# Weight maxima through TensorE instead of POOL, x tiles loaded first, and a loop jump at another place

## The chip, the cores and the metric

The kernel runs on one core of one Trainium2 chip. The metric is the device time of one execution in microseconds (us); the time given is the median of three runs. Profiles come from one execution taken by the hardware profiler. The core has five engines with queues of their own: TensorE (PE, with its weight loads as PEld), VectorE (DVE), ScalarE (ACT), GpSimd (POOL) and SyncE (SP), which here only issues DMAs. Engines wait for one another on semaphores.

## What is computed

```python
def reference(x, w_qkv, w_out, b_out, w_gate, w_up, w_down):      # x: (8, 1024, 512)
    xn = layernorm(x)
    return x + attn(xn, w_qkv, w_out, b_out) + ffn(xn, w_gate, w_up, w_down)

def attn(x, ...):                       # 8 heads of 64, windows of 4 tokens, stride 2
    win = (x @ w_qkv)[:, idx]           # idx: window starts 0, 2, 4, ... plus 0..3
    q, k, v = split(win)
    o = softmax(q @ k.T * C ** -0.5) @ v          # inside each window and head
    return scatter_add(zeros, idx, o @ w_out + b_out)

def ffn(x, ...):                        # 512 -> 1408 -> 512
    gate, up = fp4_linear(x, w_gate), fp4_linear(x, w_up)
    return fp4_linear(silu(gate) * up, w_down)
    # fp4_linear rounds both operands to FP4 (E2M1) in blocks of 16 with a scale per block
```

## The kernel before

x is 8 batches of 8 tiles of 128 tokens. The first part of the program makes the attention, batch by batch, and prepares the FFN's weights beside it; the second part makes the FFN, 64 tiles in one pipeline. The products of the projections take f16 pairs: an operand is split into a high and a low half, and three products (high-high, high-low, low-high) stand for one. One projection step is 12 products of 512 columns.

**The order** of each engine's work is a string of steps, written out by hand or by a planner: `q3` is step q number 3 of the present batch, `q3+` the same of the next batch, `q3'` of the previous one. `batches` (line 116) follows four strings: a head, then a loop of six turns whose body is two of the strings, then a tail. Where the body ends, the engine jumps back. Every engine has its own strings; they meet only in semaphores.

**Steps on TensorE:** `q` and `v` project q/k and v (L970, L977, products at L960), `s` makes scores of three tiles (L1004), `a` attends (L1021), `p` projects out (`prj`, L960), `F` is a third of the gate and up products of the first FFN tile, `W` waits until w_out and the edge rows are ready. The `q` and `v` steps go through three PSUM buffers `acc`, so each needs ACT's copy of the third step before it.

**VectorE:** `t` statistics of an x tile (L691, L694), `n` normalisation (L780), `Q` maximum over one of four row blocks of w_qkv (L650), `W0` maximum over the four (L639), `W1` the gain from it (`weight_gain`, L629 to L633), `V` low half of a sixth of the weights (L657), `U` the same three steps for w_out, `M` maxima of the nine chunks of the FFN's weights (L819), `G` their gains, `m`, `c`, `k`, `u`, `z` the softmax of three tiles, `w` the transposition of the spread weights (L749), `A`, `R` rounding of FFN weights, `I`, `J` rounding of the first FFN rows.

**ACT:** `x` high half of a normalised tile, `W` high half of a sixth of the weights (L863), `q`, `v` copies from PSUM (L884, L891), `e` exponential, `o` and `h` attention output. The first copy waits for all six `V`, since the raw weights lie in `qk`.

**POOL:** `r` the root of four tiles' variances (L538 and after), `l` low half of a tile, `w` spreading of weights (L561), `b` bias, `o` low half of the output, `C` loads of constants. `W` and `T` are the all-reduces: a maximum lies in one number per partition after VectorE, and `partition_all_reduce` (L528, L601) brings the maximum over all 128 partitions into each.

**SP:** `l` load of an x tile, `k` store of a normalised one, `t` transposing DMA of a tile's halves into `xt`, `C` w_out, `M` a chunk of FFN weights, `e` edge rows, `r`, `s` residual and output. The four parts of w_qkv are issued from ACT's queue, at its start.

Of the kernel before, what the change touches and what calls it, by code (L numbers as in the profile page):

```python
# [8 lines left out]
ALU = mybir.AluOpType  # L9
# [6 lines left out]
P = 128  # L16
# [242 lines left out]
def attention(nc, ctx, x, w_qkv, w_out, b_out, w_gate, w_up, w_down, small, part, normed, ready, late, wsc, raw,  # L259
# [48 lines left out]
    tops = sb("tops", [P, 9])  # L308

# [76 lines left out]
    def sync(sp):  # L386
# [109 lines left out]
        def first_edge(b, n):  # L496
# [15 lines left out]
                {"l": load, "k": keep, "e": edge_values, "r": residual, "s": store,  # L512
                 "L": load_unit, "S": keep_unit, "M": load_maxima, "Z": load_ready,
                 "C": load_out_weights, "W": first_edge, "I": first_rows, "t": turn_rows, "T": turn_unit, "X": turn_first})
    def gpsimd(pool):

        def load_constants(b, n):
            if n == 0:
                pool.dma_start(cst[:, :], small).then_inc(c_in, 16)
# [5 lines left out]
        def all_max(b, n):  # L525

            pool.wait_ge(w_max, n)
            pool.partition_all_reduce(sc[:, 2 * n - 1:2 * n], sc[:, 2 * n - 2:2 * n - 1], P,  # L528
                                      bass.bass_isa.ReduceOp.max).then_inc(w_all, 1)
            if n == 2:  # L530
                pool.wait_ge(bias_set, 3)
# [73 lines left out]
        batches(pool,  # L605
# [800 lines left out]
```

## Time and profile before

| | |
|---|---|
| median of 3 runs | 2263.82 us (2260.72 to 2269.66) |
| the profiled execution's own time | 2262.21 us |
| its span | 2260.4 us |
| granted TensorE clock, mean | 0.988 |
| TensorE busy | 2171.7 us, 96 % |
| VectorE, ACT, POOL busy | 72 %, 29 %, 54 % |
| attention | up to about 890 us |
| FFN | from there to the end |

The span runs from the first to the last recorded instruction. The clock is given as a share of 2.4 GHz; 0.50 is 1.2 GHz. A group of equal instructions in a timeline is one row, with its start, the time to the end of the last, the count, and in brackets the idle time ahead of it with what ended it. "issue" stands where nothing in the profile ended it. A float32 product shows as two instructions in the trace, so a score step of 96 products has 192 rows' worth of instructions, and an attend step of 16 has 32.

### The profile page before, as it was taken

The numbers are of one execution on the slowest core, as the hardware profiler recorded it, in microseconds if no ns is written. First come the engines' busy times: TensorE is split into PE (matmuls) and PEld (weight loads), VectorE is DVE, ScalarE is ACT, GpSimd is POOL, SyncE is SP. The second block draws the span as 40 slices with busy tenths as digits, with TensorE's granted clock in tenths as the row PEclk, the third lists the DMA queues.
The fourth block names the chain that finished last, engine by engine and source line by source line (L and its number), as shares of the span: only waits on it lengthen the run. The fifth ranks groups of instructions, "written<-read, shape, count | busy, mean of one in ns | idle before, by whom it ended". The sixth has DMA issues, their size and how long they took to land.

```text
span 2260.4 us, 46863 instructions
## 1 busy us (share of the span) xinstructions
PE 2171.7 (96%) x16704; PEld 1048.6 (46%) x16704; DVE 1637.1 (72%) x3099; ACT 655.9 (29%) x1009; POOL 1217.9 (54%) x880
## 2 busy tenths in 40 slices
PE   3899999999999998999999999999999999999999
PEld 1444444444445444444444444444444444444444
DVE  6587676766767555777778778778778778778774
ACT  2233333332333322222222222222222222222221
POOL 2166566665756445555555555555555555555553
PEclk9999999999999999999999999999999999999999
DMA  7656465655656635333433433333333333333432
GB/s 221 183 127 182 120 177 135 152 142 136 167 123 176 148 104 192 75 79 79 94 80 78 92 81 80 89 81 83 87 84 82 85 83 79 89 81 76 94 69 70
DMA packets 449389, 251.84 MB, mean 111 GB/s; under 512 B 367266, under 2 KB 373922, under 8 KB 449268
## 3 DMA queue, kind: packets, MB, share of 16 engines
q1 hardware_dynamic: 448404, 245.94, 44.6%
q10 hardware_dynamic: 576, 3.15, 0.3%
q8 instruction: 101, 1.65, 0.3%
q0 software_dynamic: 288, 0.94, 0.2%
q14 instruction: 20, 0.16, 0.0%
HBM read 98.98 MB, written 59.77 MB: 70 GB/s over the span
## 4 chain that ended last, share of the span: by engine, by line
PE 88%; issue 5%; DVE 3%; POOL 1%; DMA 1%; ACT 1%; SPq 0%; DVEq 0%; ACTq 0%; POOLq 0%
PE acc L960 19%; PE prj L1316 7%; PE ops L1316 7%; PE prj L960 6%; PE acc L1297 5%; PE acc L1298 5%; PE acc L1301 5%; PE ops L1318 3%; PE prj L1318 3%; PE acc L1299 2%; PE acc L1300 2%; PE acc L1302 2%; PE sps L1302 2%; PE sps L1300 2%; PE sps L1299 2%
## 5 line engine op out<-in xcount | busy, mean ns | idle before, releaser
L960 PE MATMUL acc<-late 128*128 128x512 f16 x2304 | 536.3, 390 | 61.0 <-DVE late L657 33.5
L960 PEld LDWEIGHTS acc<-late 128*128 128x128 f16 x2304 | 223.9, 100 | 339.6 <-issue 92.5
L208 POOL TENSOR_TENSOR qk<-qk,xh 128x1408 f32<-128x1408 f32 x64 | 165.6, 2588 | 230.1 <-DVE qk L245 230.1
L203 POOL TENSOR_TENSOR qk<-qk,xh 128x1024 f32<-128x1024 f32 (+1 forms) x128 | 177.3, 1385 | 111.2 <-DVE xh L224 111.2
L213 POOL TENSOR_TENSOR v<-qk,v 128x1408 f16<-128x1408 f32 x64 | 183.0, 2859 | 100.3 <-ACT v L255 100.3
L1191 DVE SCALAR_TENSOR_TENSOR qk<-acc,row_gains,xh 128x512 f32<-128x512 f32 x64 | 48.0, 750 | 253.1 <-ACT xh L1256 253.1
L1316 PE MATMUL prj<-late,qk 128*128 128x512 f16 x704 | 214.6, 379 | 0.7 <-DMA qk<-v 0.7
L1316 PE MATMUL ops<-late,qk 128*128 128x512 f16 x704 | 214.6, 379 | 0.0
L1297 PE MATMUL acc<-late,turned 128*128 128x512 f16 x512 | 194.4, 380 | 3.0 <-DVE qk L1191 3.0
L255 ACT ACTIVATE v<-qk 128x1408 f16<-128x1408 f32 x64 | 88.1, 1377 | 367.4 <-POOL qk L208 367.4
L1298 PE MATMUL acc<-late,turned 128*128 128x512 f16 x512 | 194.4, 380 | 0.0
L1301 PE MATMUL acc<-late,turned 128*128 128x512 f16 x512 | 194.3, 380 | 0.0
L960 PE MATMUL prj<-wo,oh 128*128 128x512 f16 x768 | 176.3, 379 | 4.8 <-DVE res L773 3.7
L250 ACT ACTIVATE qk<-qk 128x1024 f32<-128x1024 f32 (+1 forms) x128 | 101.1, 790 | 226.5 <-POOL qk L203 226.5
L208 POOL TENSOR_TENSOR raw<-raw,scales 128x512 f32<-128x512 f32 x64 | 67.8, 1060 | 141.7 <-DVE raw L245 141.7
L1318 PE MATMUL prj<-late,qk 128*128 128x512 f16 x352 | 133.5, 379 | 0.0
L1318 PE MATMUL ops<-late,qk 128*128 128x512 f16 x352 | 133.4, 379 | 0.0
L553 POOL TENSOR_TENSOR res<-res,bias 128x512 f32<-128x512 f32 x64 | 83.3, 1305 | 66.9 <-DMA res<-in_L_attn_x 66.8
L1256 ACT ACTIVATE xh<-acc,row_gains 128x512 f32<-128x512 f32 x128 | 83.7, 677 | 121.5 <-PE sps L1302 120.3
L884 ACT ACTIVATE qk<-acc 128x512 f32<-128x512 f32 x128 | 74.8, 593 | 148.0 <-PE acc L960 143.7
L245 DVE SCALAR_TENSOR_TENSOR qk<-qk 128x1024 f32<-128x1024 f32 (+1 forms) x128 | 114.1, 891 | 4.4
L960 PEld LDWEIGHTS prj<-wo,oh 128*128 128x128 f16 x768 | 73.2, 98 | 93.0 <-issue 5.7
(150 smaller groups left out, 4422.5 us busy)
## 6 DMA issues: line engine op xcount, KB each, us to landing
late<-in_L_attn_x SPq DMA_DIRECT2D x64, 256.0 KB, 3.8
normed<-late SPq DMA_DIRECT2D x64, 256.0 KB, 3.0
res<-in_L_attn_x SPq DMA_DIRECT2D x64, 256.0 KB, 3.1
attended<-res SPq DMA_DIRECT2D x64, 256.0 KB, 2.5
raw<-normed SPq DMA_DIRECT2D x64, 256.0 KB, 2.7
v<-attended SPq DMA_DIRECT2D x64, 256.0 KB, 2.7
out<-v SPq DMA_DIRECT2D x64, 256.0 KB, 2.0
ready<-turned SPq DMA_DIRECT2D x36, 256.0 KB, 2.7
```

What stands on the lines that cost most here:

```text
L203: pool.tensor_tensor(blocks(v), blocks(v), spread(s[2]), ALU.mult).then_inc(q["scaled"], 1)
L208: pool.tensor_tensor(blocks(v), blocks(v), spread(s[3]), ALU.mult).then_inc(q["valued"], 1)
L213: pool.tensor_tensor(h[:, 1], v, h[:, 0], ALU.subtract).then_inc(q["low"], 1)
L245: dve.scalar_tensor_tensor(v, m, ROUND_MIN, v, ALU.max, ALU.subtract).then_inc(q["rounded"], 1)
L250: act.activation(m, v, ACT.Abs, scale=ROUND_Y).then_inc(q["rounder"], 1)
L960: last = pe.matmul(out, lhsT, rhs, start=(at == 0), stop=(at == n - 1))
L1297: pe.matmul(g, x_hi, g_hi, start=(c == 0), stop=False)
L1298: pe.matmul(g, x_hi, g_lo, start=False, stop=False)
L1299: pe.matmul(w, x_hi, u_hi, start=(c == 0), stop=False)
L1301: pe.matmul(g, x_lo, g_hi, start=False, stop=(c == KC - 1))
L1316: last = pe.matmul(dps[k][:, :], ht[:, k, at], w_hi, start=(at == 0), stop=(at == 2 * FC - 1))
L1318: pe.matmul(dps[k][:, :], ht[:, k, at], w_lo, start=False, stop=False)
```

## The change

1. The maximum over partitions is made by TensorE. VectorE multiplies an identity by the column of 128 partial maxima (`diag`), TensorE multiplies a matrix of ones by that diagonal, which puts all 128 numbers side by side into every partition of `prj`, and VectorE reduces them there. So it is for w_qkv (`M0`), w_out (`M1`) and the two FFN maxima (`M2`). POOL has no all-reduce any more. New: `eye` (loaded by POOL at its start), `ones`, `diag`.
2. ACT's queue starts with x tiles 2 and 3 and two of the four parts of w_qkv; SP's queue loads tiles 0, 1, 4 and 5, then stores the first normalised tile, then loads the other two parts (`Q`).
3. The semaphores' first increments are made by POOL and not by TensorE.
4. All heads and tails have a new order. The loop's body is the same sequence on each engine; TensorE's jump back stands ahead of `q3+` instead of ahead of `q5+`.

```diff
@@ sync
+        def load_weights(b, k):
+            sp.dma_start(wqs[:, k], w_qkv[k * P:(k + 1) * P, :]).then_inc(w_in[k], 16)
-                "l0 l1 l2 l3 k0 l4 l5 l6 l7 t0 t1 t2 t3 k1 k2 k3 C0 M0 M1 t4 t5 l0+ l1+ M2 M3 t6 k4 l2+ l3+ M4 t7 M5 "
+                "l0 l1 l4 l5 k0 Q2 Q3 l6 t0 t1 l7 t2 t3 k1 C0 M0 M1 l0+ t4 k2 l1+ l2+ l3+ l4+ k3 k4 k5 t5 t6 M2 t7 M3 "
@@ gpsimd
+                pool.dma_start(eye[:, :], ident).then_inc(c_in, 16)
-        def all_max(b, n):
-            pool.wait_ge(w_max, n)
-            pool.partition_all_reduce(sc[:, 2 * n - 1:2 * n], sc[:, 2 * n - 2:2 * n - 1], P,
-                                      bass.bass_isa.ReduceOp.max).then_inc(w_all, 1)
-        def all_tops(b, n):
-            for n in range(2):
-                pool.wait_ge(m_top, n + 1)
-                pool.partition_all_reduce(wsc[:, 2 + n:3 + n], wsc[:, n:n + 1], P,
-                                          bass.bass_isa.ReduceOp.max).then_inc(m_all, 1)
+        for q, n in per_batch.items():
+            pool.sem_inc(q, n)
@@ vector
+        dve.memset(ones[:, :], 1.0).then_inc(half_set, 1)
         def weight_gain(n):
+            at_ = n // 2 * P
             dve.wait_ge(w_all, (n + 1) // 2)
+            link(dve.tensor_reduce(sc[:, n:n + 1], prj[:, at_:at_ + P], AX.X, ALU.max))
@@ weights, n == 0
                 dve.wait_ge(wq_max, KC)
-                dve.tensor_reduce(sc[:, 0:1], sc[:, 16:20], AX.X, ALU.max).then_inc(w_max, 1)
+                dve.tensor_reduce(sc[:, 0:1], sc[:, 16:20], AX.X, ALU.max).then_inc(wq_max, 1)
+                dve.wait_ge(c_in, 32)
+                dve.wait_ge(wq_max, KC + 1)
+                dve.tensor_scalar(diag[:, 0], eye[:, :], sc[:, 0:1], None, ALU.mult).then_inc(w_max, 1)
...
+        def unit_tops(b, n):
+            dve.wait_ge(m_done, 9)
+            dve.wait_ge(w_all, 2)
+            for n, cols in enumerate((slice(0, 6), slice(6, 9))):
+                dve.tensor_reduce(wsc[:, n:n + 1], tops[:, cols], AX.X, ALU.max).then_inc(m_step, 1)
+                dve.wait_ge(m_step, n + 1)
+                dve.tensor_scalar(diag[:, n], eye[:, :], wsc[:, n:n + 1], None, ALU.mult).then_inc(m_top, 1)
@@ scalar
-        for k in range(KC):
+        for i in range(2, 4):
+            act.dma_start(xb[:, i, :], x_t[i]).then_inc(x_in[i], 16)
+        for k in range(2):
             act.dma_start(wqs[:, k], w_qkv[k * P:(k + 1) * P, :]).then_inc(w_in[k], 16)
@@ tensor
-        for q, n in per_batch.items():
-            pe.sem_inc(q, n)
+        def column_tops(b, n):
+            if n < 2:
+                pe.wait_ge(half_set, 2)
+                pe.wait_ge(w_max, n + 1)
+                pe.matmul(prj[:, n * P:(n + 1) * P], ones[:, :], diag[:, n], start=True, stop=True).then_inc(w_all, 1)
+            else:
+                pe.wait_ge(m_top, 2)
+                for m in range(2):
+                    pe.matmul(prj[:, (2 + m) * P:(3 + m) * P], ones[:, :], diag[:, m],
+                              start=True, stop=True).then_inc(m_all, 1)
-                "q0 q1 q2 q3 q4 q5 q6 q7 v0 s0 v1 v2 v3 q8 q9 q10 q11 q12 q13 q14 q15 v4 v5 s1 a0 v6 v7 a1 s2 a2 q0+ "
-                "q1+ q2+ q3+ q4+ a3 W0",
-                "p6' v4 s1 a0 v5 a1 p7' v6 s2 v7 a2 q0+ q1+ q2+ a3 q3+ q4+",
-                "q5+ a4 q6+ q7+ v0+ p0 a5 v1+ s0+ p1 a6 v2+ p2 a7 v3+ q8+ q9+ q10+ q11+ p3 q12+ q13+ p4 a8 q14+ p5 "
+                "M0 q0 q1 q2 q3 q4 q5 q6 q7 v0 v1 v2 M1 s0 v3 q8 q9 q10 q11 q12 q13 q14 q15 v4 v5 s1 a0 M2 v6 v7 a1 "
+                "s2 a2 q0+ q1+ q2+ W0 a3",
+                "p6' v4 s1 a0 v5 a1 p7' v6 s2 v7 a2 q0+ q1+ q2+ a3",
+                "q3+ q4+ q5+ a4 q6+ q7+ v0+ p0 a5 v1+ s0+ p1 a6 v2+ p2 a7 v3+ q8+ q9+ q10+ q11+ p3 q12+ q13+ p4 a8 "
```

TensorE's queue, from its start to the loop (`L119` is the loop's entry; L960 and L1004 are products of projections and scores, L1021 of attending). Before:

```order
L960 MATMUL acc<-late 128x512 x108
L1004 MATMUL sps<-qk 32x32 x96
L960 MATMUL acc<-late 128x512 x156
...
L1021 MATMUL ops<-pt,v 64x64 x16
L960 MATMUL acc<-late 128x512 x24
L1021 MATMUL ops<-pt,v 64x64 x16
L1004 MATMUL sps<-qk 32x32 x96
L1021 MATMUL ops<-pt,v 64x64 x16
L960 MATMUL acc<-late 128x512 x60
L1021 MATMUL ops<-pt,v 64x64 x16
L119 UNCONDITIONAL_BRANCH
```

The same stretch of the changed kernel, where L977, L1021 and L1038 are those lines and L1054, L1058 the products with ones:

```order
L1054 MATMUL prj<-diag,ones 128x128
L977 MATMUL acc<-late 128x512 x132
L1054 MATMUL prj<-diag,ones 128x128
L1021 MATMUL sps<-qk 32x32 x96
L977 MATMUL acc<-late 128x512 x132
...
L1038 MATMUL ops<-pt,v 64x64 x16
L1058 MATMUL prj<-diag,ones 128x128 x2
L977 MATMUL acc<-late 128x512 x24
...
L1038 MATMUL ops<-pt,v 64x64 x16
L977 MATMUL acc<-late 128x512 x36
L1038 MATMUL ops<-pt,v 64x64 x16
L119 UNCONDITIONAL_BRANCH
```

The score step s0 moved behind two more projection steps, four products with ones came in, and 24 products (q3+, q4+) left the stretch between the second `s2` and the loop.

POOL's queue at its start (L538 is the root, L547 a low half, L528 the all-reduce, L519 and L522 loads). Before:

```order
L538 TENSOR_SCALAR ln<-mv 128x4
L540 TENSOR_TENSOR ln<-ln,sc 128x4
L543 TENSOR_SCALAR ln<-ln 128x4
L547 TENSOR_TENSOR xh<-late,xh 128x512 x4
L519 DMA cst<-in_small 128x291
L528 ISA
L528 ISA sc<-sc 128x1
L522 DMA bias<-in_L_attn_b_out 128x512 x3
L538 ISA
L538 TENSOR_SCALAR ln<-mv 128x4
```

The changed kernel:

```order
L525 DMA eye<-in_ident 128x128
L526 DMA cst<-in_small 128x291
L541 ISA
L541 TENSOR_SCALAR ln<-mv 128x4
L543 TENSOR_TENSOR ln<-ln,sc 128x4
L546 TENSOR_SCALAR ln<-ln 128x4
L550 TENSOR_TENSOR xh<-late,xh 128x512 x3
L529 DMA bias<-in_L_attn_b_out 128x512 x3
L550 TENSOR_TENSOR xh<-late,xh 128x512
L541 TENSOR_SCALAR ln<-mv 128x4
```

Between the first root and the second there is no all-reduce and no `ISA` step any more, and the constants are loaded ahead of the first root.

## Rows read from the trace of the kernel before

**Rows 1.** The page's first part: an engine's busy time, share, instructions.

```profile
PE 2171.7 (96%) x16704; PEld 1048.6 (46%) x16704; DVE 1637.1 (72%) x3099; ACT 655.9 (29%) x1009; POOL 1217.9 (54%) x880
```

**Rows 2.** Waits of TensorE: waiter, releaser, us in total, times, longest.

```profile
PE acc L960 <- DVE late L657: 33.5, 1, 33.5
PE acc L960 <- issue: 23.8, 8, 4.1
PE sps L1004 <- issue: 8.8, 7, 1.7
```

**Rows 3.** Timeline, 12 to 63 us: start, length, engine, instruction, count, idle before.

```profile
12.73 0.69 DVE L691 BATCH_NORM_STATS2 st<-late 128x6 f32<-128x512 f32 x1 [1.55 <-DMA late<-in_L_attn_x]
13.57 0.18 DVE L694 BATCH_NORM_AGGREGATE mv<-st 128x2 f32<-128x6 f32 x1
16.11 0.55 DVE L780 TENSOR_SCALAR late<-late,mv,ln 128x512 f32<-128x512 f32 x1 [0.72 <-POOL ln L543]
19.67 3.40 DVE L650 TENSOR_REDUCE sc<-qk 128x1 f32<-128x1536 f32 x2
24.85 0.12 DVE L639 TENSOR_REDUCE sc<-sc 128x1 f32<-128x4 f32 x1
29.56 0.38 POOL L528 PARTITION_ALL_REDUCE sc<-sc  x1 [5.77 <-issue]
31.94 7.24 DVE L657 SCALAR_TENSOR_TENSOR late<-qk,sc,late 128x1024 f16<-128x1024 f32 x6
33.45 12.51 PE L960 MATMUL acc<-late 128*128 128x512 f16 x48 [33.45 <-DVE late L657]
45.30 0.25 POOL L538 TENSOR_SCALAR ln<-mv 128x4 f32<-128x4 f32 x1 [13.65 <-issue]
49.55 13.11 PE L960 MATMUL acc<-late 128*128 128x512 f16 x60 [3.59 <-ACT qk L884]
```

**Rows 4.** Timeline, 69 to 110 us.

```profile
69.57 35.46 PE L960 MATMUL acc<-late 128*128 128x512 f16 x151 [3.97 <-issue]
92.40 0.54 DVE L780 TENSOR_SCALAR late<-late,mv,ln 128x512 f32<-128x512 f32 x1 [4.33 <-POOL ln L543]
93.92 1.75 DVE L819 TENSOR_REDUCE tops<-ot 128x1 f32<-128x1536 f32 x1
108.76 0.71 DVE L749 STREAM_TRANSPOSE pt<-pw 128x512 f32<-128x512 f32 x1 [6.06 <-POOL pw L561]
109.62 1.13 PE L1021 MATMUL ops<-pt,v 64*64 64x64 f32 x32 [2.84 <-DVE pt L749]
```

**Rows 5.** Timeline of TensorE in the loop's first and third turn.

```profile
214.03 2.66 PE L1004 MATMUL sps<-qk 64*32 64x32 f32 x190
218.36 0.29 PE L1004 MATMUL sps<-qk 64*32 64x32 f32 x2 [1.68 <-issue]
218.59 4.35 PE L960 MATMUL acc<-late 128*128 128x512 f16 x12
241.43 4.45 PE L960 MATMUL acc<-late 128*128 128x512 f16 x12 [4.08 <-issue]
...
419.09 1.67 PE L960 MATMUL acc<-late 128*128 128x512 f16 x7 [0.33 <-issue]
...
430.35 0.24 PE L1004 MATMUL sps<-qk 64*32 64x32 f32 x2 [0.93 <-issue]
430.53 2.76 PE L960 MATMUL acc<-late 128*128 128x512 f16 x12
```

**Rows 6.** The page's DMA queues (packets, MB, share) and issues (KB each, us to landing).

```profile
q8 instruction: 101, 1.65, 0.3%
late<-in_L_attn_x SPq DMA_DIRECT2D x64, 256.0 KB, 3.8
```

**Rows 7.** Busy time of each engine in a stretch, then granted clock, DMA share, GB/s.

```profile
219.00:221.00 2.00, 2.00 (x6) 0.73 (x5) 0.00 (x0) 0.00 (x0) 0.54 (x1) 0.50 1.03 262
```

**Rows 8.** Timeline of TensorE at the start of the FFN.

```profile
914.37 0.38 PE L1297 MATMUL acc<-late,turned 128*128 128x512 f16 x1 [3.04 <-DVE qk L1191]
```

More of the change, by code:

```diff
@@ L255, in high, with attention @@
     act.activation(h[:, 0], v, ACT.Copy).then_inc(q["high"], 1)
-def attention(nc, ctx, x, w_qkv, w_out, b_out, w_gate, w_up, w_down, small, part, normed, ready, late, wsc, raw,
+def attention(nc, ctx, x, w_qkv, w_out, b_out, w_gate, w_up, w_down, small, ident, part, normed, ready, late, wsc, raw,
               rows, shared, held):
@@ L663, in out_weights @@
                 dve.wait_ge(o_in, 16)
-                dve.tensor_reduce(sc[:, 2:3], wos, AX.XY, ALU.max, apply_absolute_value=True).then_inc(w_max, 1)
+                dve.tensor_reduce(sc[:, 2:3], wos, AX.XY, ALU.max, apply_absolute_value=True).then_inc(wq_max, 1)
+                dve.wait_ge(wq_max, KC + 2)
+                dve.tensor_scalar(diag[:, 1], eye[:, :], sc[:, 2:3], None, ALU.mult).then_inc(w_max, 1)
             if n == 1:
@@ L681, in fixed_values @@
             else:
-                dve.wait_ge(c_in, 16)
+                dve.wait_ge(c_in, 32)
                 dve.wait_ge(b_in, 48)
@@ L819, in maxima @@
             dve.tensor_reduce(tops[:, n:n + 1], v, AX.XY, ALU.max, apply_absolute_value=True).then_inc(m_done, 1)
+        def unit_tops(b, n):
[5 more added lines that the diff above has]
+                dve.tensor_scalar(diag[:, n], eye[:, :], wsc[:, n:n + 1], None, ALU.mult).then_inc(m_top, 1)
         def unit_gains(b, n):
-            dve.wait_ge(m_done, 9)
-            dve.tensor_reduce(wsc[:, 0:1], tops[:, 0:6], AX.X, ALU.max).then_inc(m_top, 1)
-            dve.tensor_reduce(wsc[:, 1:2], tops[:, 6:9], AX.X, ALU.max).then_inc(m_top, 1)
             dve.wait_ge(m_all, 2)
+            for n in range(2):
+                dve.tensor_reduce(wsc[:, 2 + n:3 + n], prj[:, (2 + n) * P:(3 + n) * P], AX.X, ALU.max)\
+                    .then_inc(m_step, 1)
+            dve.wait_ge(m_step, 4)
+            dve.wait_ge(m_top, 2)
             dve.tensor_scalar(wsc[:, 0:2], wsc[:, 2:4], 1.0 / 6.0, 1e-12, ALU.mult, ALU.max).then_inc(m_step, 1)
-            dve.wait_ge(m_step, 1)
+            dve.wait_ge(m_step, 5)
             dve.tensor_scalar(wsc[:, 2:4].bitcast(I32), wsc[:, 0:2].bitcast(I32), 0x7F800000, None,
                               ALU.bitwise_and).then_inc(m_step, 1)
-            dve.wait_ge(m_step, 2)
+            dve.wait_ge(m_step, 6)
             dve.reciprocal(wsc[:, 6:8], wsc[:, 2:4]).then_inc(m_step, 1)
@@ L850, in vector @@
                  "A": unit_scales, "R": round_unit,
-                 "M": maxima, "G": unit_gains, "W": weights,
+                 "M": maxima, "G": unit_tops, "H": unit_gains, "W": weights,
                  "Q": weights_top, "V": weights_low, "U": out_weights, "Z": fixed_values,
@@ L1035, in out_ready @@
             pe.wait_ge(ve_zero, 16)
+            pe.wait_ge(m_step, 4)
         def first_products(b, n):
@@ L1041, in tensor @@
         batches(pe,
-                "q0 q1 q2 q3 q4 q5 q6 q7 v0 s0 v1 v2 v3 q8 q9 q10 q11 q12 q13 q14 q15 v4 v5 s1 a0 v6 v7 a1 s2 a2 q0+ "
-                "q1+ q2+ q3+ q4+ a3 W0",
-                "p6' v4 s1 a0 v5 a1 p7' v6 s2 v7 a2 q0+ q1+ q2+ a3 q3+ q4+",
-                "q5+ a4 q6+ q7+ v0+ p0 a5 v1+ s0+ p1 a6 v2+ p2 a7 v3+ q8+ q9+ q10+ q11+ p3 q12+ q13+ p4 a8 q14+ p5 "
-                "q15+",
-                "q5 q6 a4' q7 a5' v0 v1 p0' s0 p1' v2 p2' a6' v3 q8 p3' q9 q10 a7' q11 q12 q13 q14 a8' p4' q15 v4 p5' "
-                "s1 v5 v6 a0 s2 a1 p6' v7 a2 p7' a3 a4 F0 a5 p0 p1 a6 p2 a7 p3 a8 p4 p5 p6 p7 F1 F2",
-                {"q": project_qk, "v": project_v, "s": scores, "a": attend, "p": project_out, "W": out_ready,
+                "M0 q0 q1 q2 q3 q4 q5 q6 q7 v0 v1 v2 M1 s0 v3 q8 q9 q10 q11 q12 q13 q14 q15 v4 v5 s1 a0 M2 v6 v7 a1 "
+                "s2 a2 q0+ q1+ q2+ W0 a3",
+                "p6' v4 s1 a0 v5 a1 p7' v6 s2 v7 a2 q0+ q1+ q2+ a3",
+                "q3+ q4+ q5+ a4 q6+ q7+ v0+ p0 a5 v1+ s0+ p1 a6 v2+ p2 a7 v3+ q8+ q9+ q10+ q11+ p3 q12+ q13+ p4 a8 "
+                "q14+ p5 q15+",
+                "q3 q4 q5 q6 q7 a4' v0 v1 p0' s0 p1' a5' v2 v3 q8 a6' p2' a7' q9 p3' a8' q10 q11 q12 p4' q13 q14 q15 "
+                "v4 a0 v5 a1 s1 p5' v6 v7 s2 a2 p6' a3 a4 p7' a5 p0 p1 a6 p2 a7 p3 a8 p4 p5 p6 p7 F0 F1 F2",
+                {"q": project_qk, "v": project_v, "s": scores, "a": attend, "p": project_out, "M": column_tops, "W": out_ready,
                  "F": first_products})
@@ L1356, in build @@
         held = sem("held")
-        att, ended = attention(nc, ctx, x, w_qkv, w_out, b_out, w_gate, w_up, w_down, small, part, normed, ready, late,
+        att, ended = attention(nc, ctx, x, w_qkv, w_out, b_out, w_gate, w_up, w_down, small, ident, part, normed, ready, late,
                                wsc, raw, rows, shared, held)
```

15 lines of the change are left out of this document (8 added, 7 removed), and 34 rows, old and new, of tables (dst, to, v).

## The prediction

> **What bounds the kernel now.** I read the busy line first, then TensorE's waits, then the timeline from the start, then the places where TensorE stops. TensorE is busy 2171.7 us of 2260.4 [rows 1]. Of what is left, 33.5 us stand before the first product, 23.8 us in 8 stops with no releaser ("issue"), 8.8 us in 7 more such stops at the scores [rows 2]. So a microsecond counts only where it takes a TensorE stop away or adds one; the other engines matter where they end such a stop. There are three kinds.
>
> *The start.* Ahead of TensorE's 33.45 stand, one after another: the fourth tile's statistics (end 13.75), the first normalisation at 16.11, the weight reductions, the one over all four at 24.97, POOL's all-reduce, over at 29.94, and the split of the weights from 31.94 [rows 3]. From 24.97 to 29.94 nothing but the all-reduce is on this path: 5.0 us.
>
> *POOL behind an all-reduce.* Its next ordinary step, root 1, comes at 45.30 after 13.65 us with no releaser. So tile 4 is normalised late, ACT has its step x4 ahead of the copies, and TensorE waits 3.59 us at 49.55 [rows 3]. Behind the third all-reduce VectorE waits 6.06 us for POOL's spreading and turns the weights at 108.76, for which TensorE waits 2.84 us at 109.62 [rows 4].
>
> *Stops with no releaser.* Five, the first of 4.08 us, stand at the loop's jump, ahead of q5. Six stand in s2, each after 190 of its 192 rows, the first of 1.68 and the third of 0.93 us [rows 5], 7.8 us in all. They recur at one instruction, so they hang on the program's place in memory and not on data. The page has a queue for instructions with 101 packets and 1.65 MB, 16.3 KB each [rows 6]. I take an instruction as 64 bytes, which makes a packet a block of 256; that is inferred, and this is its test. A row of the timeline is two instructions, load and product. From the stop at 419.09, after 5 of v5's 12 products, to the one at 430.35, after 190 rows of s2 [rows 5], there are 7 + 32 + 12 + 12 + 190 = 253 rows, 506 instructions, and 7 waits and register steps: 513, two blocks and one. The stop at 69.57 [rows 4], after 5 products of v1, lies 13 x 256 ahead of the one at 419.09 by the same count. So TensorE stops where two block borders follow each other faster than a block arrives. In s2 they are 128 rows apart, 1.8 to 1.9 us at its rate (190 rows in 2.66); with the stops of 0.93 to 1.68 a block takes 2.8 to 3.5 us.
>
> *The clock.* From 219 to 221 the granted clock is 0.50, that is 1.2 GHz [rows 7], behind the stop of 1.68, and v7's 12 products take 4.35 us; behind that of 0.93 they take 2.76 [rows 5]. Such a fall costs 1.6 us.
>
> **The change, part by part.** *x ahead of weights.* An x tile lands 3.8 us after its issue [rows 6], so the first at 4.6; VectorE takes about 1.0 a tile (12.73 to 13.75), and the first normalisation was 2.36 behind the fourth aggregate [rows 3]: 4.6 + 4.0 + 2.4 = 11. Four of them take 2.1 (0.55 each), four weight reductions 6.8 (3.40 for two): 20. SP now issues two of the four weight parts behind the first normalised tile, at 12. They are three x tiles' bytes each; between 3.8 and three times that I take 6, so they are there at 18, and at worst at 23. Tile 6 ends at 21, the reduction over all with it; before, 24.97.
>
> *TensorE for POOL.* The 5.0 us become a 128x128 multiply, one f32 product and one reduction from PSUM. No row shows these; the nearest are VectorE's 128x512 step of 0.55 and its 128x1536 reduction of 1.7, and f16 products of 0.23 to 0.36. With their semaphores I bound the three by 0.8 and 2.5 us. They lie beside tile 7's statistics and root 1, for the first split now has tile 4's normalisation ahead of it: tile 7 at 22.3 to 23, 2.36 to the root's end, 0.55 for tile 4, makes 25.2 to 25.9 against 31.94. I take 25.9: **6.0 us**, 3 (late weights) to 7.
>
> *No reload on POOL.* Root 1 comes at once and x4 is past before the first copy, so the 3.59 goes. At a0 the spreading comes straight behind VectorE's first group, some 30 us ahead of TensorE: the 2.84 goes. **6.4 us**, and 1.6 of a clock fall behind the latter, of which I take **0.8**. What is late next there: TensorE's queue now holds M1 ahead of s0 and M2 behind a0, and it waits in them for VectorE, with v6, v7, a1, s2 and all later work queued behind M2. M1 comes at 62.66 (49.55 + 13.11) - 9.6 + 5.2 = 58; the w_out maximum it needs is eleven short steps behind the last split (39.18 before, 33 now): by 48. M2 comes at 109.62 - 12 = 98; the ninth maximum ends at 95.67 even with today's order, and VectorE stood still for POOL for 4.33 us shortly ahead of it [rows 4]: about 88. The products and their weight loads cost 0.1 to 0.9 us each, three of them on the path: a loss of **1.0**.
>
> *The stop of 3.97 in the head* [rows 4]: the borders now fall 128 rows before the end of s0 and at its end, without the 5 products between. It becomes 1.0 (a block in 2.8) to 5.1 (as slow as now): no change taken.
>
> *The loop.* Every engine keeps its order; TensorE's jump alone moves, from behind q4 to behind a3. The head has 24 products less, POOL does the increments for TensorE, and the M products come in. Counted in the built program, the loop's top goes from instruction 2240 to 2158, and q5, s2 and all else of the body to 28 instructions earlier. The border that lay 4 instructions before s2's end falls 24 behind it, after 11 of v7's 12 products. Between it and the one before lie 117 rows of s2, 1.6 us, and 11 products, 2.4 us: 4.0 us where a block takes 2.8 to 3.5. So **the six stops of s2 go, 7.8 us**, and with them falls of the clock. The two rows behind such stops show 1.6 and none; for the six I take four falls, 6.4, less 1.5 since the jump's stop may now be the one that halves it for longer: **4.9**. The jump's stop stays: its target block must still come. Sum 12.7, 7 (clock as now) to 15.
>
> *The tail.* F0, which filled TensorE between a4 and a5, moves behind p7, and VectorE prepares the first rows of FFN earlier. The last and largest of the tail's stops is 3.04, in the first FFN tile [rows 8]. F0's 24 products, 5.2 us, are missing as filler, while VectorE has some 5 us less between s2 and a6, and the 3.04 gets more work ahead of it: a gain of 1 to 4. Against it, by the count, s0 and s1 of the tail now hold two borders each, 128 rows apart, where none did: 2 x 1.4 us and up to two falls of the clock, 3.2. Net a **loss of 2**, from a gain of 3 to a loss of 6.
>
> **Sum.** 6.0 + 6.4 + 0.8 - 1.0 + 12.7 - 2.0 = 22.9 off the profiled run's 2262.21 us (its span is 2260.4) gives 2239.3. That run is 1.6 under the median of the runs, 2263.82, so the same off the median is 2240.9.
>
> The Trainium skill's page "Runtime: NRT & Kernel Launch", section "Instruction fetch mechanics", has blocks of 16 KiB, 256 instructions, whose fetch is mostly hidden behind issue, and a stall where a taken branch leaves the window. The packets of rows 6 and the stop at the jump agree with it. The stops in s2 speak against "hidden", as nothing branches there; taken at its word they have another cause and stay, which is rival 1.
>
> The Trainium skill's page "GPSIMD Engine Reference", section "Instruction dispatch", states about 6 us ahead of a freshly loaded kernel's first call. The 5.0 us ahead of the first all-reduce are near that; the 13.65 behind it are twice as long, and the sum goes by the rows.
>
> **Rivals.** (1) *The s2 stops are no borders, or do not move.* The loop gives nothing, the tail's new stops do not come either: 6.0 + 6.4 + 0.8 - 1.0 + 1 = 13 off, 2251. For it: the block is inferred. Against: three kinds of stops at whole multiples of 256. (2) *The head's gain is lost again*, at M1, M2 or through late weights: TensorE is 12 us ahead there, and VectorE has to be so too. With the loop's gain alone: 10.7 off, 2253. (3) *The jump's block comes slowly.* The jump moves 5 us forward, into a stretch with transfers under way. If the block takes as in the head, 3.97 + 1.8 + 1.1 = 6.9 us, the five stops grow by 3.4 each, with falls of the clock by 5: 1 off, 2263. (4) *Slower: M2 waits.* Its place is TensorE's queue behind a0; each us that the ninth maximum ends after 98 costs one. Its loads wait in turn for reductions, SP has edge rows and transposes between them, and VectorE waits at the w_out gain for M1. Against 22.9 it makes the kernel slower than now from 121, by over 0.5 % from 132, which gives 2275. Against it: 95.67 today.
>
> **How the numbers follow.** Forecast with its ends, 2231 to 2249: 0.62. More gain: 0.04. Rival 1, 2249 to 2254: 0.16. Rival 2, 2250 to 2256: 0.10. Rival 3: 0.05. Rival 4: 0.03. An effect of 0.5 % is 11.3 us, about what a measurement of this kernel can tell from no change; faster is below 2252.5. Of rival 1 three quarters lie there, of rival 2 half: 0.62 + 0.04 + 0.12 + 0.05 = 0.83, same 0.14, slower 0.03. The range 2230 to 2254 leaves out about 0.15.
>
> **What the profile after must show.** TensorE's first product with weights at 26 to 29; no stop of 3.6 at the first copies and none at a0, which comes at about 98; no 13 us gap on POOL. In the loop no stop in s2, and one of 3.7 to 4.1 at the jump, ahead of q3. In the tail one stop inside s0 and one inside s1, so the stops at scores sum to about 5 us, not 8.8. Wrong would be a wait at M1 or M2, or s2's stops still at 190 of 192.

## The result, and the profile after

The changed kernel takes **2241.03 us** (median of 4 runs, 2238.1 to 2243.07) against 2264.56 for the kernel before, ratio 0.9901 with a 95% interval of 0.9879 to 0.9923. The prediction said 2241. Its profiled run took 2239.38 us with a span of 2237.6, against 2262.21 and 2260.4. Of the four executions each of two kernels further down, one with the jump back (2292.88) and one with the late bias loads (3253.32) ran slower at a lower granted clock; they count in those medians and not in the ratios.

The total came as forecast, the parts did not. I cut both spans at the same three places of TensorE: its first product with weights, attend a4 of the head, and attend a4 of the tail. Tail and FFN stay one row, since the change moves F0 from one to the other. "Stopped" is the stretch less TensorE's busy time in it.

| stretch | before | after | difference | of it stopped | of it busy | forecast |
|---|---|---|---|---|---|---|
| to the first product | 33.45 | 35.96 | +2.5 | | | -6.0 |
| head, to a4 | 105.21 | 96.59 | -8.6 | -6.7 | -2.0 | -6.2 |
| loop, a4 to a4 | 633.12 | 618.08 | -15.0 | -7.6 | -7.4 | -12.7 |
| tail and FFN | 1488.6 | 1487.0 | -1.7 | +1.6 | -3.3 | +2.0 |
| sum | | | -22.8 | | | -22.9 |

The page's first line (busy us, share of the span, instructions) and TensorE's waits (waiter, releaser, us in total, times, longest), which answer to [rows 1] and [rows 2]:

```profile
PE 2159.8 (97%) x16712; PEld 1048.1 (47%) x16712; DVE 1640.4 (73%) x3108; ACT 655.2 (29%) x1009; POOL 1216.9 (54%) x877
```

```profile
PE acc L977 <- issue: 22.9, 6, 4.4
PE prj L1054 <- DVE diag L643: 22.8, 1, 22.8
PE acc L977 <- DVE late L661: 12.4, 1, 12.4
...
PE ops L1038 <- issue: 3.8, 2, 2.3
...
PE sps L1021 <- issue: 2.3, 1, 2.3
```

TensorE's busy time fell by 12 us although its record has 8 rows more, those of the four products with ones. Its mean granted clock rose from 0.988 to 0.994, so most of that is half-clock time that is gone. The stops at the scores went from 8.8 us in 7 to 2.3 in one; those ahead of the large products hardly moved (23.8 to 22.9). The start, in the timeline (start, length, engine, line, operation, count, idle time before and what ended it), answers to [rows 3]:

```profile
14.44 5.76 SPq L408 DMA_TRANSPOSE late<-xh  x2
20.25 0.58 SPq L395 DMA_DIRECT2D late<-in_L_attn_x  x1
21.01 9.59 SPq L408 DMA_TRANSPOSE late<-xh  x2
```

```profile
22.15 0.12 DVE L640 TENSOR_REDUCE sc<-sc 128x1 f32<-128x4 f32 x1
22.38 0.29 DVE L643 TENSOR_SCALAR diag<-eye,sc 128x128 f32<-128x128 f16 x1
30.92 0.69 DVE L697 BATCH_NORM_STATS2 st<-late 128x6 f32<-128x512 f32 x1 [8.25 <-DMA late<-in_L_attn_x]
...
31.85 0.26 DVE L629 TENSOR_REDUCE sc<-prj 128x1 f32<-128x128 f32 x1
```

The maxima are spread as meant: diagonal at 22.38, product, one reduction. But VectorE stands 8.25 us ahead of that reduction for the eighth x tile. Its load was issued at 20.25, behind two transposing DMAs that took 5.76 us to issue. Next the head behind it, answering to [rows 4]:

```profile
35.96 30.22 PE L977 MATMUL acc<-late 128*128 128x512 f16 x132 [12.38 <-DVE late L661]
66.02 0.38 PE L1054 MATMUL prj<-diag,ones 128*128 128x128 f32 x2
66.33 1.82 PE L1021 MATMUL sps<-qk 64*32 64x32 f32 x192
70.42 30.07 PE L977 MATMUL acc<-late 128*128 128x512 f16 x132 [2.27 <-issue]
...
102.41 0.69 PE L1038 MATMUL ops<-pt,v 64*64 64x64 f32 x32
103.03 0.71 PE L1058 MATMUL prj<-diag,ones 128*128 128x128 f32 x4
...
114.06 0.56 PE L1038 MATMUL ops<-pt,v 64*64 64x64 f32 x13 [2.27 <-issue]
```

No stop at the first copies, none at a0, no wait at M1 or M2. The stop behind s0 is 2.27 instead of 3.97, and the one inside a2 is 2.27 instead of 0.69. The loop's first turn answers to [rows 5]:

```profile
207.40 2.83 PE L1021 MATMUL sps<-qk 64*32 64x32 f32 x192
210.16 2.76 PE L977 MATMUL acc<-late 128*128 128x512 f16 x12
...
221.36 0.69 PE L1038 MATMUL ops<-pt,v 64*64 64x64 f32 x32
226.44 4.02 PE L977 MATMUL acc<-late 128*128 128x512 f16 x10 [4.39 <-issue]
```

s2 runs through, in every turn; the jump, now ahead of q3, has its stop: 4.39, 4.08, 4.11, 4.01 and 4.08 us in the five times that it is taken. Five such stops, 20.7 us, are nearly all that TensorE stands still in the loop (618.08 less 597.05 busy). In the tail there is one stop in s1 and none in s0, and the FFN's first one, [rows 8], is 0.44 instead of 3.04:

```profile
812.26 0.26 PE L1021 MATMUL sps<-qk 64*32 64x32 f32 x5 [2.32 <-issue]
...
893.14 0.38 PE L1327 MATMUL acc<-late,turned 128*128 128x512 f16 x1 [0.44 <-DVE qk L1221]
```

So two questions stood: why the start was 8.5 us later than forecast, and whether the program's place in memory is really what makes the stops.

### The profile page after: what moved, and what is told of

The parts are those of the page before. It is cut to its first block, busy times and chain, and to the rows that moved or that the text cites. A ratio compares the mean times of both kernels' runs of the same rounds, so it can differ in the third digit from the quotient of the medians.

```text
span 2237.6 us, 46878 instructions
## 1 busy us (share of the span) xinstructions
PE 2159.8 (97%) x16712; PEld 1048.1 (47%) x16712; DVE 1640.4 (73%) x3108; ACT 655.2 (29%) x1009; POOL 1216.9 (54%) x877
## 4 chain that ended last, share of the span: by engine, by line
PE 94%; DVE 2%; issue 2%; DMA 1%; ACT 0%; POOL 0%; SPq 0%; DVEq 0%; ACTq 0%; POOLq 0%
PE acc L977 23%; PE prj L977 7%; PE prj L1346 7%; PE ops L1346 7%; PE acc L1327 5%; PE acc L1328 5%; PE acc L1331 5%; PE ops L1348 3%; PE prj L1348 3%; PE sps L1021 2%; PE sps L1332 2%; PE acc L1332 2%; PE sps L1330 2%; PE acc L1330 2%; PE acc L1329 2%; PE sps L1329 2%
## 5 line engine op out<-in xcount | busy, mean ns | idle before, releaser
L977 PE MATMUL acc<-late 128*128 128x512 f16 x2304 | 526.1, 387 | 35.3 <-issue 22.9
L977 PEld LDWEIGHTS acc<-late 128*128 128x128 f16 x2304 | 223.3, 99 | 307.3 <-issue 54.9
L977 PE MATMUL prj<-wo,oh 128*128 128x512 f16 x768 | 176.3, 379 | 5.7 <-DVE res L779 5.7
L550 POOL TENSOR_TENSOR xh<-late,xh 128x512 f16<-128x512 f32 x64 | 77.0, 1213 | 101.6 <-ACT xh L894 101.5
L977 PEld LDWEIGHTS prj<-wo,oh 128*128 128x128 f16 x768 | 73.2, 98 | 93.7 <-issue 5.5
```

What stands on the lines that cost most here:

```text
L977: last = pe.matmul(out, lhsT, rhs, start=(at == 0), stop=(at == n - 1))
```

## Experiments

All ratios are against the kernel before in the same comparison, with 95% intervals. "Waits" are waits of TensorE on a semaphore that has long been set; they only move the rest of its program on. The built program keeps half of the repeated ones: 228 written move it by 114 instructions, 60, 28 and 28 by 30, 14 and 14, and the traces hold just so many instructions more (46977 against 46863; 46908, 46892 and 46892 against 46878). My first two expectations had counted all of them.

### The kernel before, its program moved on

```diff
+        for _ in range(228):
+            pe.wait_ge(half_set, 1)
```

> The kernel before, with 228 waits that are already fulfilled put at the start of TensorE's queue, where it stands idle for 33 us. All else is the kernel before. They move every later TensorE instruction 228 on in memory, which is 28 back against block borders of 256, as the change does. If the stops in s2 come from two borders 128 rows apart (theory of borders): no stop at row 190 of s2 in the six turns, turns of about 103 us instead of 105.5, the first weight product still at 33.5, and the whole 12 to 16 us faster than the kernel before, ratio 0.993 to 0.995. If they come from the data, from the jump's place or from what runs beside s2 (rival): stops where they were, ratio 1.000 within 0.002.

Measured: 2276.14 us, ratio 1.0077 (1.0055 to 1.0098). The direction was missed. TensorE's waits, and one stop of the second turn:

```profile
PE sps L1006 <- issue: 39.9, 19, 3.4
```

```profile
256.44 2.00 PE L1006 MATMUL sps<-qk 64*32 64x32 f32 x180
261.09 0.28 PE L1006 MATMUL sps<-qk 64*32 64x32 f32 x12 [2.64 <-issue]
```

The stops behind row 190 of s2 are gone, and others stand in s0 behind row 180 and in s1 behind row 174, of every turn. With the shift corrected to 114, the same count of 256 instructions puts two borders 128 rows apart there, so that two steps of a turn have a stop instead of one. One place does not fit: the border at row 190 of s2 should have moved to row 133, 128 rows behind another, and in the six turns s2 has no stop but one of 0.23 us. So the count places the stops that came, while two borders 128 rows apart did not always make one; why not there, no run shows. And a second thing: the stop at the jump, 4.08 us in [rows 5], is gone (one of 0.40 is the largest that I read there). Nothing at the jump had been touched, so the jump's stop depends on place as well, which the prediction had not thought of.

### The changed kernel, its program moved on

```diff
+        for _ in range(28):
+            pe.wait_ge(half_set, 1)
```

> The changed kernel with 28 fulfilled waits at the start of TensorE's queue, where it stands idle. Borders fall 28 instructions earlier in the work, so that in the loop they are where they were before the change. Theory of borders: in each turn a stop of 0.9 to 1.7 us after 190 of 192 rows of s2, with falls of the clock, turns of about 105 us, and 12 to 16 us more than the changed kernel: ratio to the kernel before 0.995 to 0.997. Rival (the jump's place, ahead of q3, took the stops away): no stop in s2, ratio 0.990.

Measured: 2243.26 us, ratio 0.9924 (0.9905 to 0.9943), which overlaps that of the changed kernel; its profiled span is 2234.2. The expectation was missed: 14 instructions are too few to bring a border back into s2. By the count the border comes to lie in v7, the step behind s2, after 4 of its 12 products, and there the stops are, 0.21 to 0.95 us in the six turns:

```profile
310.48 1.04 PE L979 MATMUL acc<-late 128*128 128x512 f16 x4
312.24 1.89 PE L979 MATMUL acc<-late 128*128 128x512 f16 x8 [0.72 <-issue]
```

### The jump back where it was

```diff
-                "s2 a2 q0+ q1+ q2+ W0 a3",
-                "p6' v4 s1 a0 v5 a1 p7' v6 s2 v7 a2 q0+ q1+ q2+ a3",
-                "q3+ q4+ q5+ a4 q6+ q7+ ...",
-                "q3 q4 q5 q6 q7 a4' v0 ...",
+                "s2 a2 q0+ q1+ q2+ W0 a3 q3+ q4+",
+                "p6' v4 s1 a0 v5 a1 p7' v6 s2 v7 a2 q0+ q1+ q2+ a3 q3+ q4+",
+                "q5+ a4 q6+ q7+ ...",
+                "q5 q6 q7 a4' v0 ...",
```

> The changed kernel with the jump of TensorE back ahead of q5: q3+ and q4+ stand in the head and at the body's end. The order of the work is the same in every engine, and s2 keeps its place against the borders within 4 instructions. Theory of borders: the jump's place is worth nothing, ratio 0.990 within 0.001, no stop in s2, five stops of about 4 us ahead of q5. Rival (moving the jump gave the gain of the loop, 15 us): ratio 0.996.

Measured: **2222.76 us**, ratio 0.9839 (0.9782 to 0.9895), outside both of the ranges that I had put down. The timeline of TensorE at the first jump:

```profile
216.50 5.35 PE L977 MATMUL acc<-late 128*128 128x512 f16 x24
222.39 2.76 PE L977 MATMUL acc<-late 128*128 128x512 f16 x12 [0.53 <-issue]
```

The two loops, of the changed kernel and of this one (stretch, us, busy us of TensorE, granted clock, DMA share, GB/s):

```profile
132.55:750.63 618.08, 597.05 (x7513) 0.98 0.61 152
```

```profile
127.22:723.51 596.29, 589.26 (x7513) 1.00 0.63 158
```

Of the 21.8 us that are gone, 14.0 are stopped time and 7.8 busy time, at a granted clock of 1.00 instead of 0.98. So the same jump costs 3.7 to 4.1 us in the kernel before, 4.0 to 4.4 in the changed kernel, and here at most 0.6. That gave a **new theory**: a jump's stop has two causes. Behind a3's last product the first block of the target takes 4.4 us to be there (221.36 + 0.69 to 226.44). With q3 and q4 ahead of the jump, 5.35 us of products cover that. But if a border comes right behind the loop's first instruction, a second block is needed at once, and the cover is too short for both. Counted in the built programs, the loop's first instruction stands 2 instructions ahead of a border in the kernel before, 144 in the first experiment, 32 here, 84 in the changed kernel.

### Two tests of that theory

First, back behind the large products as here, but moved on by 30 instructions, so that 2 instructions are left to the border as in the kernel before:

```diff
+        for _ in range(60):
+            pe.wait_ge(half_set, 1)
```

> The kernel with the jump put back behind the large products, and TensorE's program moved on by 15 instructions more than one (60 fulfilled waits, of which the built program keeps 30), so that the first instruction of the loop again stands 2 instructions ahead of the border of a block, as in the kernel before, and the borders in the turns again stand where they stood in it. Theory A (a jump's stop has two causes: a block that lies beyond a border just behind the loop's first instruction, and large products missing ahead of the jump to cover the fetch): the stop at the jump returns, 3.5 to 4.1 us in each of 6 turns, and s2's stop after 188 to 190 rows, 1.3 to 1.7 in each turn; 6 x (3.8 + 1.4) = 31 us on jump_back's 2222.8, so 2250 to 2256, ratio 0.994 to 0.998. Theory B (it was only the step that the jump stands ahead of): no stop at the jump, ratio 0.984 to 0.988 with s2's stops alone.

Measured: 2251.32 us, ratio 0.9971 (0.9952 to 0.9991), as theory A said.

```profile
206.85 2.72 PE L1023 MATMUL sps<-qk 64*32 64x32 f32 x190
211.15 0.25 PE L1023 MATMUL sps<-qk 64*32 64x32 f32 x2 [1.58 <-issue]
...
224.84 5.35 PE L979 MATMUL acc<-late 128*128 128x512 f16 x24
233.98 5.30 PE L979 MATMUL acc<-late 128*128 128x512 f16 x12 [3.79 <-issue]
```

Both kinds of stops of the kernel before are back at their rows: at the five jumps 3.79, 3.31, 4.70, 3.25 and 3.87, and behind row 190 of s2 six of 0.99 to 1.58. Fulfilled waits ahead of all work, which do nothing, cost 28.6 us by the medians, 1.3% by the ratios.

Second, the kernel before with the jump's place as the only edit:

```diff
-                "q1+ q2+ q3+ q4+ a3 W0",
-                "p6' v4 s1 ... q0+ q1+ q2+ a3 q3+ q4+",
-                "q5+ a4 q6+ ...",
-                "q5 q6 a4' q7 ...",
+                "q1+ q2+ a3 W0",
+                "p6' v4 s1 ... q0+ q1+ q2+ a3",
+                "q3+ q4+ q5+ a4 q6+ ...",
+                "q3 q4 q5 q6 a4' q7 ...",
```

> The kernel before with one part of the change alone: the jump of TensorE's loop ahead of q3 (behind attend a3) instead of ahead of q5. The loop's first instruction comes to stand 54 ahead of a border instead of 2; the borders within the turns stay where they were. Theory A: the cover is gone (a3's small products take 0.7 us) while the border is no longer near, so one stop takes the place of the other: 3.8 to 4.5 us ahead of q3, s2's stops stay at 1.3 to 1.7, ratio 0.999 to 1.003. Theory B (only the border just behind the loop's first instruction makes the stop): no stop at the jump, 6 x 4.1 = 24.5 us less, ratio 0.988 to 0.990.

Measured: 2265.44 us, ratio 1.0031 (1.0011 to 1.0052); theory B is out.

```profile
236.98 0.69 PE L1021 MATMUL ops<-pt,v 64*64 64x64 f32 x32
241.75 9.54 PE L960 MATMUL acc<-late 128*128 128x512 f16 x36 [4.07 <-issue]
```

One cause took the place of the other: 3.42 to 4.07 us at each of the five jumps, where it had been 3.69 to 4.08 with a border behind the loop's first instruction.

A look at the size: jump back, and 18 instructions left to the border.

```diff
+        for _ in range(28):
+            pe.wait_ge(half_set, 1)
```

> jump_back with TensorE's program moved on by 14 instructions (28 fulfilled waits, of which the built program keeps half): the loop's first instruction stands 18 ahead of a border, between jump_back's 32 (stops of 0.3 to 0.7) and jump_back_shifted's 2 (3.3 to 4.7). If the products between the loop's first instruction and the border cover the second block's fetch, 7 products of 0.22 us less stand there than at 32: the stops at the jump are 1.5 to 2.3 us; the span 2212.9 plus 6 x 1.4 = 2221. If the effect has a threshold instead, they are as at 32 or as at 2.

```profile
220.86 6.93 PE L979 MATMUL acc<-late 128*128 128x512 f16 x31
228.74 1.24 PE L979 MATMUL acc<-late 128*128 128x512 f16 x5 [0.94 <-issue]
```

Measured, in one execution: 2222.28 us, span 2220.1. The 31 products are q3, q4 and 7 of q5's 12: behind every jump TensorE runs 7 products into q5 and stops there, 0.94, 1.82, 1.82, 1.27 and 0.99 us, which is the border itself, seen in the trace. In four of the turns a further 0.5 to 1.0 stands ahead of q5. Together they are 0.9 to 2.9 us, where I had expected 1.5 to 2.3; they lie between those of the other two places, so at this one place neither of the two sizes of a threshold came.

The stops can also be laid beside the transfers of instructions, since the trace has a time for every packet of queue q8 of [rows 6]. Inside the stop at the first jump it has one, in the kernel before (237.35 to 241.43):

```profile
q8 instruction: 1, 0.02, 2.2%
```

and in the changed kernel (222.05 to 224.40; from there to 226.44 it has none):

```profile
q8 instruction: 1, 0.02, 3.3%
```

In the kernel before the packet in the stop, from 238.50 to 239.93, is the second behind the jump: the first runs from 234.44 to 236.30, while q3 and q4 still multiply. In the changed kernel the first, from 223.32 to 224.56, stands in the stop itself. With the jump back it runs from 219.51 to 220.39, beneath q3 and q4 (216.50 to 221.85). These are the two causes of the theory. And it holds for all stops: up to 900 us, the profiles of the thirteen kernels have 136 stops of TensorE of 0.9 us or more with no releaser, and each of them ends 1.2 to 2.1 us after a packet of this queue has landed. Only about 11% of the time lies so behind a packet. So they are waits for instructions on their way.

### The start: what made x7 late

The queues from 20 to 32 us, of the changed kernel (packets, MB, share of the 16 engines' time), and the median landing there of the transposing DMAs, 12.5 us against 4.0 in the kernel before:

```profile
q1 hardware_dynamic: 3923, 1.21, 65.9%
q0 software_dynamic: 240, 0.79, 46.6%
...
late<-xh SPq DMA_TRANSPOSE x3, 12.5
```

The queue q0 carries POOL's three bias loads, which the change issues at 16.62 and the kernel before at 29.82. They broadcast one row to 128 partitions. Two edits tell the bias loads and the issue order of SP apart:

```diff
-                "C0 r0 l0 l1 l2 C1 l3 r1 l4 l5 ...      (POOL)
+                "C0 r0 l0 l1 l2 l3 r1 l4 C1 l5 ...
```

> The changed kernel with POOL's three bias loads behind its low half of tile 4 instead of behind that of tile 2. In the changed kernel x tile 7, behind two transposing DMAs, lands 10.6 us after its issue and holds the weights' gain until 31.75. Theory A: the bias loads (0.79 MB in small packets, 47 % of the DMA engines from 20 to 32 us) crowd out the transposes; without them tile 7 is there at 22 to 24, TensorE's first weight product at 26 to 28 instead of 35.96, and the whole 7 to 10 us faster than the changed kernel, ratio 0.986 to 0.987. Theory B: the transposes are slow beside any transfer, tile 7 at 28 or later, gain under 3 us, ratio 0.989 to 0.990.

```diff
-                "l0 l1 l4 l5 k0 Q2 Q3 l6 t0 t1 l7 t2 t3 ...      (SP)
+                "l0 l1 l4 l5 k0 Q2 Q3 l6 l7 t0 t1 t2 t3 ...
```

> The changed kernel with one edit of order: SP issues the load of the eighth x tile ahead of the first two transposing DMAs; the bias loads stay where the change put them. Theory A (x7 was late because its issue stood behind 5.8 us of transposing issues): VectorE's wait of 8.25 for it falls to 2 to 3 and the first weight product comes at 29 to 31; ratio 0.987 to 0.990. Theory B (it was late because the bias loads filled the queues, wherever it is issued): the first weight product stays at 34 to 36, ratio 0.990.

Measured with the bias late: first product at 27.93, in line with theory A for the start; 2234.94 us, ratio 0.9893 (0.9836 to 0.9949), the profiled span 6.9 shorter. The ratio itself lies in theory B's range and can't be told from the changed kernel's 0.9901; what decides is the trace.

```profile
20.51 2.66 SPq L408 DMA_TRANSPOSE late<-xh  x2
...
22.90 0.69 DVE L697 BATCH_NORM_STATS2 st<-late 128x6 f32<-128x512 f32 x1 [0.66 <-DMA late<-in_L_attn_x]
```

Measured with x7 early: first product at 31.03, at the upper end of theory A; 2235.88 us, ratio 0.9899 (0.9874 to 0.9924). VectorE no longer waits for x7 (its statistics start at 22.25), but now TensorE waits for a transposed tile, since the four transposes take 13 us to issue:

```profile
14.87 13.03 SPq L408 DMA_TRANSPOSE late<-xh  x4
```

```profile
31.03 30.98 PE L977 MATMUL acc<-late 128*128 128x512 f16 x132 [7.79 <-DMA late<-xh]
```

So the order alone is half of it; the bias loads under way slow whatever transposes stand beside them. Moving the bias took the two later transposes from 9.59 us of issuing to 2.66. How the bias loads slow them is open. It is not how busy the engines are: with the bias late, the packets from 20 to 32 us take 104.5% of the engines' time, as against 112.5%, and the transposes land in 3.4 us. No run took the loads out altogether.

### What POOL's all-reduces cost by themselves

```diff
-            pool.partition_all_reduce(sc[:, 2 * n - 1:2 * n], sc[:, 2 * n - 2:2 * n - 1], P,
-                                      bass.bass_isa.ReduceOp.max).then_inc(w_all, 1)
+            pool.tensor_copy(sc[:, 2 * n - 1:2 * n], sc[:, 2 * n - 2:2 * n - 1]).then_inc(w_all, 1)
```

> The kernel before with POOL's three all-reduces left out: an ordinary copy on POOL stands in the place of each, so every partition is scaled by its own maximum, and the output isn't the reference's. All orders, waits and TensorE's program stay as before. It leaves in the jump, the s2 stops and the old order of loads, so it prices what the all-reduces and POOL's idle time behind them cost. Theory A, as in the prediction: 5.0 us at the start (first weight product at 28.5 to 29.5) and the stops of 3.59 at the first copies and 2.84 at a0 gone, with a little less clock loss: 10 to 13 us earlier at a4 of the head, ratio 0.994 to 0.996. Rival (the head's time is set by something else, DMA of x tiles or VectorE, once POOL is out of the way): under 6 us, 0.998 or more.

Measured: 2252.0 us, ratio 0.996 (0.9948 to 0.9972). POOL's gap of 13.65 us is gone, its next step comes 1.29 us behind VectorE's; a4 of the head comes 4.2 us earlier, not 10 to 13. The ratio fits theory A's 0.994 to 0.996, the head fits the rival's "under 6 us"; since theory A was about the head, it missed.

```profile
62.52 34.10 PE L958 MATMUL acc<-late 128*128 128x512 f16 x151 [4.07 <-issue]
...
101.38 0.27 PE L1019 MATMUL ops<-pt,v 64*64 64x64 f32 x1 [2.01 <-issue]
...
114.99 1.12 PE L1019 MATMUL ops<-pt,v 64*64 64x64 f32 x28 [3.69 <-issue]
```

The start gained 3.8 (first product at 29.62, by then held by a transposed tile). Behind it nothing was gained: 104.9 us to a4, as 105.2 before. The stops of 3.59 and 2.84 for other engines went, and at the same borders of the program 2.01 us came up inside a0 and 3.69 instead of 0.69 inside a2; with the 3.97 that is now 4.07 the sum of the four is 9.8 instead of 11.1, and TensorE's busy time is 1.0 us more, at a granted clock of 0.93 instead of 0.95. One of these the instruction queue shows: in the kernel before, a packet runs from 106.63 to 107.72, inside the wait of 2.84 for VectorE (106.78 to 109.62); here one runs from 98.88 to 99.86, and the stop of 2.01 stands around its landing. So that wait had hidden a block on its way. For the stop in a2 I infer the like.

### Both findings together

The changed kernel with the jump back and the bias late, and the same with x7 early too:

> The changed kernel with the jump back behind q3 and q4, and POOL's three bias loads behind the low halves of x5's tile. If the two add: first weight product near 28 instead of 36, no stop over 0.7 us at the jumps; jump_back's 2222.8 less the 5 to 7 that the earlier start left in the span, 2215 to 2218, ratio 0.979 to 0.982. If the late bias costs something later that the jump's stops hid (a wait of DVE for bias, or x tiles that come late for a loop without stops): 2220 to 2224, ratio 0.982 to 0.985.

> As jump_back_bias, and the load of the eighth x tile ahead of the first two transposing DMAs in SP's order. Theory A (x7's tile, DVE's last work ahead of the weight gain, was late behind the two transposes): the first weight product at 25.5 to 27, 1 to 2 us ahead of the run with the bias alone, ratio 0.978 to 0.981. Rival: the transposes come later by what x7 takes, and the first product waits for their tiles: at 28 or later, no gain.

Measured: **2212.04 us**, ratio 0.9801 (0.9777 to 0.9825), and 2212.76 us, 0.9796 (0.9768 to 0.9824). The ratio is in the range that I gave for "the two add". By the intervals only the jump's part is clear of noise: that of the late bias alone, 0.9836 to 0.9949, lies above this one, while that of the jump back alone, 0.9782 to 0.9895, overlaps with it. In the profiles the start's part shrinks: against the jump back alone the first product comes 6.4 us earlier (28.26 for 34.65), a4 of the head 2.2 (125.06 for 127.22). x7's place makes no difference that can be measured here, though the first product comes at 27.22 instead of 28.26, between theory A's range and the rival's. TensorE's waits in the first of them:

```profile
PE acc L977 <- issue: 5.4, 4, 3.8
...
PE ops L1038 <- issue: 4.6, 5, 1.6
PE acc L977 <- DMA late<-xh: 2.4, 3, 1.1
PE sps L1021 <- issue: 2.2, 2, 2.0
```

This is the version that beats both kernels, by 2.0% and about 1.0%. What is left of stops with no releaser is 12.2 us; waits for transposed tiles now show in the loop, at up to 1.1 us.

## Why the prediction was right, and where only its sum was

**The start (forecast -6.0, measured +2.5) was the step that failed.** The working put tile 7's statistics at 22.3 to 23; they came at 30.92. The weights, which it had as the uncertain part, were there: the reduction over all at 22.15, where it said 21. It had costed x tiles by their mean landing of 3.8 us and had not costed the two things the change puts ahead of and beside the eighth tile: SP's transposes in the issue order and POOL's bias loads, now 13 us earlier. With the bias late the same step gives 22.90, the first split is at 26.40 (forecast 25.9) and the first product at 27.93.

**The products on TensorE (forecast a loss of 1.0)** took 0.38 and 0.71 us on the path, 1.1, and no wait at M1 or M2. Rival 4 had no footing.

**No reload on POOL (forecast 7.2 with its clock).** Both stops went, 6.4 us, as forecast. That they gave a gain of that size hung on the program's place: in the kernel before with the all-reduces alone taken out, the same two stops went and the head, counted from its first product, got no shorter. The missing sentence in the step is "what is late next there", asked of the instruction stream: the prediction asked it of VectorE only. **The stop of 3.97** became 2.27, inside its 1.0 to 5.1; the stop in a2 grew by 1.6, not forecast. These cancel. Of the head's 8.6 the rest, 2.0, is less half-clock time, net of the new products.

**The loop (forecast -12.7, measured -15.0).** The mechanism held: s2's stops, 7.8 us, are gone as forecast; the five at the jump take 20.7 us for 19.4, and with smaller gaps the stopped time fell by 7.6. Busy time fell by 7.4, which I put down to the clock (granted 0.98 for 0.97), where 4.9 was put; that term was sized too low, since I had feared the jump's stop would lower the clock for longer. That place in the program makes these stops is now shown and not only counted: moving the program put them at rows 180 and 174, after product 4 of v7, and back at row 190, and each ends behind a packet of instructions. Rival 1 is out.

**"The jump's stop stays: its target block must still come"** was right in size, 4.0 to 4.4, and wrong in reason. The stop of the kernel before came from a border 2 instructions behind the loop's first; the 28 instructions by which the change moves the program would have freed it. The change's own move of the jump, from behind 24 large products to behind a3's small ones, put a second cause in its place. I had seen the move and given it nothing, because I never asked what covers the fetch. It costs the changed kernel 18.3 us by the medians (2241.03 against 2222.76) and 21.8 us of the profiled loop. The intervals of these two ratios just overlap (0.9879 to 0.9923, 0.9782 to 0.9895); with the bias late in both they do not (0.9836 to 0.9949, 0.9777 to 0.9825).

**The tail (forecast +2.0, measured -1.7)** lies in its range. One stop in s1 came as counted (2.32, and one of 1.57 in a2), the one in s0 did not, and the FFN's 3.04 shrank to 0.44, inside the gain of 1 to 4 put for it. No run took the tail apart, so how much F0's place did is open.

One error of 8.5 us that was too hopeful, at the start, met three that were too careful: 2.4 in the head, 2.3 in the loop, 3.7 in tail and FFN. The forecast of 2241 is to be read as right about the loop's borders and lucky in its sum. Of the signs it asked for, the first product at 26 to 29 (35.96), a0 at about 98 (102.41) and a stop inside s0 of the tail (none) did not come.

The Trainium skill's page "Runtime: NRT & Kernel Launch", section "Instruction fetch mechanics", calls the crossing of a block mostly hidden and the taken branch the stall. For the FFN, where products of 512 columns follow each other and no such stop stands, the traces agree. In scores, 128 rows in 1.8 us, they do not: crossings cost 0.9 to 3.4 us there. And the jump's stall, 4.1 us, was hidden down to 0.5 by large products ahead of it, so here it was not the branch that had to go but the cover that had to stay.

## What to carry to other kernels

Where stops with no releaser recur at one row, suspect the program's place in memory: see whether a packet of the instruction queue lands just ahead of their ends, count instructions between them, look for multiples of the block, and before trusting any gain of under 1% move the program by a few idle instructions and measure again. Put a loop's jump behind the longest work that is queued on its engine, and keep instructions between the loop's first one and the next border: in these kernels 32 left stops of at most 0.7 us, 18 left 0.9 to 2.9, and 2 left 3.3 to 4.7. When a wait is removed, ask also what it was hiding in the instruction stream; when loads are moved ahead, cost every DMA that is issued in front of them or travels beside them, the small broadcasts too.

## What the runs showed of the hardware

- Thirty instructions that do nothing made one kernel 28.6 us slower by the medians (2222.76 to 2251.32), 1.3% by the ratios.
- All 136 stops of 0.9 us or more with no releaser, in thirteen profiles, end 1.2 to 2.1 us after a packet of the instruction queue has landed.
- In the changed kernel a jump's target takes 4.0 to 4.4 us behind the last small product, when it is one block (226.44 less 222.05 at the first), and, in the kernel moved on by 30 instructions, with a second border right behind its first ones, 9.1 us behind a3 (233.98 less 224.84), of which q3 and q4 fill 5.35.
- A stop of 4 us at the jump also costs clock: without it the loop's busy time is 7.8 us less for five jumps, at a granted clock of 1.00 instead of 0.98.
- Three small bias broadcasts, 0.79 MB of packets from 20 to 32 us, held 46.6% of the DMA engines' time there, while transposing DMAs beside them landed in 12.5 us instead of 4.0 in the kernel before and 3.4 with the bias late.
